# Four scatters of routed tokens spread over GpSimd's queue in an attention, graph and expert kernel

## The reference

```python
h = feats @ gnn_w[l] + gnn_b[l]
h = einsum('bij,bjd->bid', adj, h) / deg
feats = gelu(h + feats)
```

## Time and profile before

| | us |
|---|---|
| median of 3 runs | 1107.71 |
| the profiled execution, its own time | 1106.61 |
| its span, first to last instruction | 1104.8 |
| TensorE matmuls busy | 1047.9 (95%) |
| VectorE busy | 870.1 (79%) |
| ScalarE busy | 781.6 (71%) |
| GpSimd busy | 510.2 (46%) |

### The profile page before, as it was taken

How to read it: one execution, slowest core, us unless ns; L and a number is a source line. 1 busy time by engine, 2 the same in 40 slices (tenths; PEclk the granted TensorE clock), 3 DMA queues, 4 the chain that set the end, 5 groups by cost and what they waited for, 6 DMA issues and landing times.

```text
span 1104.8 us, 28275 instructions
## 1 busy us (share of the span) xinstructions
PE 1047.9 (95%) x8576; PEld 852.4 (77%) x8576; DVE 870.1 (79%) x3624; ACT 781.6 (71%) x2176; POOL 510.2 (46%) x658
## 2 busy tenths in 40 slices
PE   4899999999999999999999999999999999999993
PEld 3777777777777777777777777878787777999993
DVE  4767888797979797979797979797979697767546
ACT  3758686868687878777778786868777776666651
POOL 4424335363636363626272727272626261656444
PEclk9899999999999999999999999999999999999997
DMA  6990000000000000000000000000000012222227
GB/s 182 406 315 1 1 10 11 8 10 8 10 8 10 8 10 8 10 8 10 8 10 8 10 8 10 8 10 8 10 8 10 1 38 73 66 64 74 59 66 232
DMA packets 51813, 50.04 MB, mean 45 GB/s; under 512 B 20569, under 2 KB 43099, under 8 KB 51760
## 3 DMA queue, kind: packets, MB, share of 16 engines
q1 hardware_dynamic: 47440, 40.91, 12.2%
q0 software_dynamic: 4320, 8.47, 2.3%
HBM read 21.23 MB, written 28.58 MB: 45 GB/s over the span
## 4 chain that ended last, share of the span: by engine, by line
PE 61%; DVE 28%; issue 5%; ACT 2%; DMA 2%; SPq 2%; DVEq 0%; POOLq 0%
PE bank L653 50%; DVE eb L1461 6%; DVE nmax L1446 6%; DVE ea L1458 3%; PE bank L796 2%; PE bank L1028 2%; DVE dT L1475 1%; PE bank L757 1%; DVE aT L1480 1%; PE bank L770 1%; PE bank L771 1%; PE bank L773 1%; ACT f1T L1178 1%; DVE z L1495 1%; DMA x_all<-in_x 1%
## 5 line engine op out<-in xcount | busy, mean ns | idle before, releaser
L516 POOL TENSOR_TENSOR ea<-ea,wgt 128x256 f32<-128x256 f32 x128 | 78.2, 611 | 317.4 <-DVE wgt L1470 297.8
L1446 DVE TENSOR_REDUCE nmax<-bank 128x1 f32<-128x128 f32 (+1 forms) x512 | 149.3, 346 | 68.5 <-PE bank L653 68.5
L1120 ACT ACTIVATE gt<-bank 128x512 f32<-128x512 f32 (+1 forms) x256 | 111.7, 493 | 39.3 <-PE bank L773 38.5
L1152 ACT ACTIVATE ea<-bank,nmax 128x128 f32<-128x128 f32 x256 | 96.2, 376 | 59.5 <-DVE nmax L1446 36.8
L518 POOL TENSOR_TENSOR eb<-eb,wgt 128x512 f32<-128x512 f32 x128 | 132.7, 1037 | 0.0
L1461 DVE SCALAR_TENSOR_TENSOR eb<-idw,ssum,eb 128x256 f32<-128x256 f32 x256 | 126.1, 530 | 0.0
L1152 ACT ACTIVATE eb<-bank,nmax 128x256 f32<-128x256 f32 x256 | 123.6, 483 | 0.0
L653 PE MATMUL bank<-gt,vnat 128*64 128x256 f32 (+1 forms) x1024 | 111.2, 336 | 11.3 <-ACT gvT L1120 10.5
L653 PE MATMUL bank<-qk 64*128 64x128 f32 (+1 forms) x1024 | 113.3, 341 | 0.0
L653 PEld LDWEIGHTS bank<-gt,vnat 128*64 128x64 f32 x1024 | 68.3, 136 | 56.8 <-issue 35.0
L544 POOL DMA_INDIRECT pairs<-zout,zin x71 | 69.9, 984 | 80.0 <-DVE zout L1964 67.7
(11 more groups left out here) (237 smaller groups left out, 3103.9 us busy)
## 6 DMA issues: line engine op xcount, KB each, us to landing
slots<-gu_lo SPq DMA_DIRECT2D x33, 520.0 KB, 14.9
zin<-slots SPq DMA_DIRECT2D x71, 65.0 KB, 1.8
got<-pairs SPq DMA_DIRECT2D x8, 512.0 KB, 6.8
zin<-in_guT SPq DMA_DIRECT2D x14, 216.0 KB, 2.9
raw_gu<-in_guT SPq DMA_DIRECT2D x8, 352.0 KB, 3.4
out<-x_all SPq DMA_DIRECT2D x8, 256.0 KB, 2.7
pairs<-zout,zin POOLq DMA_INDIRECT x71
dn<-in_downT SPq DMA_DIRECT2D x2, 512.0 KB, 15.8
```

The source lines that it names most:

```text
L516: nc.gpsimd.tensor_tensor(ea[:, s], ea[:, s], wgt[:, s, 0:2].unsqueeze(2).to_broadcast([P, 2, P]), ALU.mult)
L1120: return nc.scalar.activation(o, i, ACT.Copy, **more)
L1152: done = nc.scalar.activation(e[:, s, a, :], score_bank(n, a)[:, TILE_SCORES[t]], ACT.Exp, bias=nmax[:, s, i:i + 1], accum_out=ssum[:, s, ...
L1446: done = V.tensor_reduce(nmax[:, n % 3, i:i + 1], score_bank(n, a)[:, TILE_SCORES[t]], X, ALU.max, negate=True)
```

## The change

The scatters keep their order, operands and semaphores. Instead of all four between the products and the degrees of pair 5, one stands in front of the degrees of pair 5, one behind them, one behind the degrees of pair 6 and one behind those of pair 7. It applies to batches 2 to 15. Nothing else changes.

```diff
                 graph(b, 5)
                 if routed is not None:
-                    for c in range(SIDE):
-                        scatter(routed, c)
+                    scatter(routed, 0)
                 degrees(b, 5)
+                if routed is not None:
+                    scatter(routed, 1)
                 graph(b, 6)
                 degrees(b, 6)
+                if routed is not None:
+                    scatter(routed, 2)
                 graph(b, 7)
                 degrees(b, 7)
+                if routed is not None:
+                    scatter(routed, 3)
                 if after is not None:
                     deviation(after, 1, 7)
```

## The result

Four runs of the changed kernel took 1118.45 to 1119.78 us, median 1119.09; the kernel before 1108.2 in four runs beside them. The ratio is 1.0099, 95% interval 1.0081 to 1.0116: slower by 1%. The forecast was 1118, range 1109 to 1124.5. The span of the profiled execution is 1116.8 against 1104.8: 12.0 more.

What follows compares the result with a forecast made beforehand. TensorE's queue was taken as the bound (61% of the chain), in places VectorE where TensorE waits for it. 13 x 0.89 - 0.67 = 10.9 us on 1106.61 gave 1117.5, by the runs' median 1118.6; forecast 1118, range 1109 to 1124.5.

Steps and rivals of the forecast that it cites:

- The start of the products: GpSimd, batch 8: pair 6's products start at 512.12 instead of 514.81, after scatter 0, degrees of pair 5 and scatter 1.
- The price at the second `z`: VectorE's first-layer sum of the second double starts at 515.26 instead of 514.31, 0.95 us late.
- The pattern of batch 1: Scatter-free batch 1, products ahead of pair 7's adjacency: `ea` to `eb` 0.59, `eb` to `z` 2.55 us, applied to changed batches.
- What arrives in the period: Batches 2 to 14: 0.95 less 0.06 made up gives 0.89 us a batch; period about 57.15.
- The meeting of the degrees with the adjacency of pair 6: Degrees of pair 5 delay VectorE there by up to 0.37 us, hidden behind scatter 1.
- Scatters beside `xh`: Scatter 1 beside VectorE's normalise taken as 1.06 us; the skill's rule would add about 0.4, 5 us in all.
- TensorE's wait: After the change, in batches 2 to 14, TensorE waits some 1.2 us for ScalarE's gelu f1T.
- Batch 15: Its 1.82 us `eb` collision goes; `z` starts at 910.58 instead of 911.25, 0.67 us gained once.
- The tail: Scatter 3 before `rstd` and the landing wait: taken as nothing; uncovered, `rstd` costs at most 0.2 us.
- The sum: Whole kernel: 13 x 0.89 - 0.67 = 10.9 us added to the profiled execution's 1106.61, giving 1117.5.
- Long collision: Rival: products start during pair 7's adjacency, as in batch 15; 1.34 x 13 = 17.4 us, time 1124; chance 0.09.
- Faster: Rival: degrees collision goes and VectorE wins the port at pair 6's products; `z` 0.37 earlier, -4.8, time 1101.8; chance 0.11.

Runs made afterwards that it cites:

- run with the wait: Changed kernel plus one wait: GpSimd starts pair 6's products only after VectorE's adjacency of pair 7; ratio 1.0043 to the kernel before.
- run with the degrees first: Kernel before with one edit: degrees of pair 5 put in front of the block of four scatters; ratio 1.0048.
- all late: Against the changed kernel, all four scatters moved into one block behind the power rstd; ratio 1.0057 to the kernel before.
- run with three and one: Against the kernel before, three scatters stay in the old place, the last goes behind the degrees of pair 7; ratio 1.0198.

## Why the prediction was right, step by step

*The start of the products.* Forecast 3.12 behind the first `z`, measured 3.13: 1.06, 0.76 and 1.01 for scatter, degrees, scatter instead of 1.06, 0.72 and 1.06. Two small misses cancel here.

*The price at the second `z`.* Forecast 0.95, measured 1.00. The pattern of batch 1 came again with `eb` product to `z` 2.61 for 2.55; the first of the last two operations took 0.54, beside the start of scatter 2.

*What arrives in the period.* Forecast 0.89, measured 0.95; the made-up part is 0.05, as batch 1 had it (0.06). 13 x 0.95 = 12.4 against the 11.6 in the sum: that is the mis-sized term, small.

*The meeting of the degrees with the adjacency of pair 6.* It took 0.34 (0.82 for 0.48), and 0.15 more on the first `ea` at the end of scatter 0, which I did not have. The start of the products is hidden from it behind scatter 1, as written. TensorE's wait for the mixed values is not: 0.28 of the 0.75 comes from here. It adds nothing to the period, because the wait for f1T ends later.

*Scatters beside `xh`.* Scatter 1 took 1.01, but `xh` came so late (518.50) that only the scatter's last 0.13 us lay beside it, so this run hardly tests whether a scatter is drawn out. The run with the wait does: there a scatter from 518.45 took 1.01 beside the normalise of 1.03. The drawn-out scatter of the Trainium skill (page "SBUF — State Buffer", section on SBUF's two separate sides) did not come in either. What was drawn out in the changed kernel is `xh`, 0.87, by the product behind the scatter, as in batch 1.

*TensorE's wait.* I had 1.2 us for f1T. It is 0.75 for the mixed values (0.18 of it there before) and 0.54 for f1T. The sum is about right, the first half was in a place that I had not named.

*Batch 15.* Forecast 0.67 gained; first to second `z` went from 8.06 to 7.36, 0.70. The way was not the one forecast: the `ea` there is held up for 1.11, and 3.15 from weights to `z` instead of 3.38.

*The tail.* Taken as nothing, and it was: `rstd` ends at 527.59 and its reader `xh` starts at 528.46, and GpSimd's wait for L1723 (now L1728) still lasts 64.2 us in 16 times, for 58.8.

*The sum.* The first `z` of batch 0, in front of anything that changed, lies 0.75 later in the profile after (59.34 against 58.59), and it lies between 58.2 and 60.1 in the ten profiles of this study. The 13 batches add 12.4. Behind the first `z` of batch 15 the new profile is 1.2 shorter, of which 0.70 is the gain forecast and the rest is not accounted for. 0.75 + 12.4 - 1.2 = 12.0 in the span, against 10.9 forecast. That the median of the runs (1119.09) lies only 1 us from the forecast is in part luck: such stretches differ by a microsecond or more between the profiles.

*The rivals.* "Long collision" did not come, but exists: two experiments fell into it. It costs more than the 1.34 that I priced it at: 1.7 to 1.8 in the period (58.01 and 57.98 against 56.26). Its condition was right: products starting when the adjacency is under way. "Faster" is refuted for this order; it came with another. Where I read a limit wrongly is in the experiments: with the first place quiet I took TensorE as the next bound and missed that the period before has no margin at the second-layer sum behind the normalise. In the run with the degrees first the second `z` came 0.39 earlier, counted from the first `z`, and the sum 0.43 later (524.49 - 513.08 = 11.41 against 519.98 - 509.00 = 10.98).

Shown by experiment: the loss is set by where GpSimd's multiplies meet VectorE's adjacency (one wait, scatters unmoved: 1.0195 to 0.9913), and most of it needs no scatter nearby (all late: 0.61 of the 0.95 in the period). The second place is shown too: with the sum moved in front of the normalise, TensorE's wait of 0.89 is gone and the period falls by 0.77. That the shared port to SBUF is the means is the Trainium skill's account (page "SBUF — State Buffer", section "Who interferes with whom"); the lengths fit it but no run separates it from another cause.

## What to carry to other kernels

Earlier work on an engine that nobody waits for can cost time through its neighbour: before moving it, look which operations of VectorE run beside GpSimd's two-input multiplies, and whether they stand on the chain. A phase of the same kernel that lacks the moved work (here batches 0 and 1) can price the move: their pattern gave 0.95 where 1.00 was measured. If a place has to be kept quiet, say so with a wait; a block of scatters that happens to lie there does it only until something moves. Then look where the delayed multiplies land: the same wait gave 1.0043 in one order of the scatters and 0.9913 in another.

## What was not expected of the hardware

- Between two GpSimd multiplies that follow each other, an operation of VectorE's adjacency gets its turn before a degrees multiply but not between the `ea` and the `eb` product: it is then held up through both, 1.82 us (batch 15 and the run with three and one) for an undisturbed 0.48. For the normalise this is not a rule: in the run with the degrees first one of its two operations took up to 2.41 us for some 0.34 undisturbed, through degrees, `ea`, `eb` and the next degrees. Why is open.
- A scatter hardly stretches the adjacency's operations beside it (`eb` 0.47 to 0.49, and 0.54 beside the start of scatter 2 in the change), but at the seam from a scatter to a multiply an operation grows before the multiply's recorded start: the first `ea` from 516.23 took 0.48 instead of 0.33 with the degrees recorded from 516.69. Between two scatters nothing grows (0.48 for the `eb` at 510.21 of the kernel before, over the seam at 510.43). So the recorded start of the multiply may be somewhat late there; no run shows it directly.
- In batch 8 the normalise of the batch before took 1.03 to 2.66 us for the 0.6 it needs. What counts is which multiplies it meets and not how many follow each other: the same unbroken run of six multiplies (4.33 us) gave 2.66 in one run and 1.48 in another. The size of the VectorE operation does not protect it: `ve`, 128x2 and 0.31 undisturbed, took 1.45 beside the products.
